# Attention maxima reduced two banks at a time, and a PE order planned with bursts of one key step

## What is computed

```python
att = jnp.einsum('bhql,bhkl->bhqk', q_for_k, k_lat) * L ** (-0.5)
causal = jnp.tril(jnp.ones((T, T), dtype=bool))
att = jnp.where(causal[None, None], att, -jnp.inf)
att = jax.nn.softmax(att, axis=-1)
y_lat = jnp.einsum('bhqk,bhkl->bhql', att, v_lat)
```

## Time and profile before

| | |
|---|---|
| median of 3 runs | 3118.36 us (3117.6 to 3118.45) |
| the profiled execution's own time | 3112.8 us |
| its span | 3111.2 us |
| PE busy / DVE busy / ACT busy, share of the span | 91% / 73% / 60% |
| attention stage | about 462 to 2246 us of the span |
| one slot of it in the steady part | 107 us |

### The profile page before, as it was taken

How to read it: one execution, slowest core, us unless ns; L and a number is a source line. 1 busy time by engine, 2 the same in 40 slices (tenths; PEclk the granted TensorE clock), 3 DMA queues, 4 the chain that set the end, 5 groups by cost and what they waited for, 6 DMA issues and landing times. The chain is left out here.

```text
span 3111.2 us, 50281 instructions
## 1 busy us (share of the span) xinstructions
PE 2844.3 (91%) x16538; PEld 1923.9 (62%) x16538; DVE 2273.6 (73%) x5659; ACT 1858.7 (60%) x3718; POOL 776.4 (25%) x701
## 2 busy tenths in 40 slices
PE   7888957999999999999999999999889997899990
PEld 5677744555555555555555555555367775799990
DVE  7999967888888888888888888888134543445443
ACT  4666632576667666666766676666535443546544
POOL 5777851010000001000110000010024444123220
PEclk9999986899999999999999999999989998899995
DMA  4666674242243234314332432340083220434316
GB/s 153 225 224 223 217 233 105 52 101 54 52 103 78 54 76 97 69 43 102 77 78 52 103 78 54 76 95 14 11 299 117 93 76 20 118 71 109 69 21 223
DMA packets 259647, 320.07 MB, mean 103 GB/s; under 512 B 70578, under 2 KB 157787, under 8 KB 258144
## 3 DMA queue, kind: packets, MB, share of 16 engines
q1 hardware_dynamic: 241760, 294.09, 33.4%
q0 software_dynamic: 17664, 23.19, 3.9%
HBM read 182.76 MB, written 143.95 MB: 105 GB/s over the span
## 5 line engine op out<-in xcount | busy, mean ns | idle before, releaser
L803 ACT ACTIVATE att_probs<-att_score_bank 128x512 f32<-128x512 f32 (+3 forms) x2560 | 1159.0, 551 | 608.5 <-PE att_score_bank L732 600.3
L840 DVE TENSOR_REDUCE att_partial_max<-att_max_bank 128x1 f32<-128x512 f32 x1536 | 1004.9, 687 | 124.3 <-PE att_max_bank L720 118.8
L720 PE MATMUL att_max_bank<-att_k_st,att_q_st 96*128 96x512 f32 (+3 forms) x2560 | 906.4, 389 | 31.8 <-DMA att_ident<-in_ident 20.9
L732 PE MATMUL att_score_bank<-att_q_st,att_k_st 98*128 98x512 f32 (+3 forms) x2560 | 924.5, 390 | 10.1 <-DMA att_q_st<-att_max_rows 7.6
L732 PEld LDWEIGHTS att_score_bank<-att_q_st,att_k_st 98*128 98x128 f32 x2560 | 481.8, 191 | 273.2 <-ACT att_probs L803 145.7
L720 PEld LDWEIGHTS att_max_bank<-att_k_st,att_q_st 96*128 96x128 f32 x2560 | 489.4, 193 | 244.7 <-DVE att_partial_max L840 100.7
L844 DVE CUSTOM_DVE_ANT_0 att_edge_sum<-att_max_bank,att_edge 128x128 f32<-128x128 f32 (+3 forms) x1024 | 482.0, 484 | 165.2 <-PE att_max_bank L720 164.7
L826 POOL TENSOR_SCALAR_AFFINE_SELECT att_probs<-att_probs 128x512 f32<-128x512 f32 x256 | 162.5, 635 | 1615.1 <-ACT att_probs L803 1615.1
L746 PE MATMUL att_acc_bank<-att_probs,att_v_st 128*32 128x512 f32 (+3 forms) x5120 | 544.2, 538 | 1.8 <-POOL att_probs L826 0.9
L210 POOL TENSOR_TENSOR proj_op_low<-proj_turned,proj_op_high 128x512 fp32r<-128x512 f32 x192 | 275.0, 1462 | 59.1 <-ACT proj_op_high L332 58.9
L746 PEld LDWEIGHTS att_acc_bank<-att_probs,att_v_st 128*32 128x32 f32 x5120 | 131.9, 109 | 245.2 <-issue 140.3
(11 more groups left out here) (221 smaller groups left out, 3887.3 us busy)
## 6 DMA issues: line engine op xcount, KB each, us to landing
qk_parts<-proj_parts SPq DMA_DIRECT2D x64, 1024.0 KB, 4.6
att_q_st<-qk_parts SPq DMA_DIRECT2D x192, 256.0 KB, 4.0
att_k_st<-qk_parts SPq DMA_DIRECT2D x192, 256.0 KB, 6.1
v_tokens<-proj_v_tok SPq DMA_DIRECT2D x64, 256.0 KB, 4.4
att_v_st<-v_tokens SPq DMA_DIRECT2D x64, 256.0 KB, 6.9
exp_w<-in_ew SPq DMA_DIRECT2D x16, 1024.0 KB, 8.9
dispatched<-mix_empty_rows SPq DMA_DIRECT2D x8, 1036.0 KB, 14.5
exp_rows<-dispatched SPq DMA_DIRECT2D x16, 518.0 KB, 5.5
```

Of the source, the lines that this page charges most:

```text
L720: nc.tensor.matmul(max_ps[u % MAXB][:, 0:width], q_st[0:3 * L, n % QBUF, j, t * P:(t + 1) * P], k_st[0:3 * L, g % 2, kb, j, 0:width], star ...
L732: nc.tensor.matmul(score_ps[h % SCOREB][:, q0:CH], k_st[:, g % 2, kt // TT, j, (kt % TT) * P:(kt % TT + 1) * P], q_st[:, n % QBUF, j, q0:C ...
L803: nc.scalar.activation(probs[:, k % PROBS, j, q0:CH], score_ps[(HG * k + j) % SCOREB][:, q0:CH], ACT.Exp).then_inc(exped, 1)
L840: nc.vector.tensor_reduce(best, bank[:], AX.X, ALU.max).then_inc(unit_reduced, 1)
```

## The change

Three edits, all in attend and its planner:

1. Units are numbered so that t and t+1 of one head and one key block are neighbours (MU). The 4 banks become 2 tensors of two neighbouring banks each. For a pair off the diagonal, one tensor_reduce over 128x2x512 gives both maxima. It waits until both units are scored, and hands back both banks when it ends. Units on the diagonal keep an instruction each.
2. The planner reckons with that: nothing on VectorE for the even unit, 2 x 512 columns at 960 per us plus 0.075 us for the odd one.
3. BURST and GATHER go from 2 to 1, and the weights of the two backlogs in a weighing's price from 0.3 to 0.1.

```diff
-MU = [(s, c, j, t, kb) for s in range(SLOTS) for c in range(NC) for j in range(HG) for t in range(TT) for kb in range(c + 1)]
+MU = [(s, c, j, t + i, kb) for s in range(SLOTS) for c in range(NC) for j in range(HG) for t in range(0, TT, 2)
+      for kb in range(c + 1) for i in range(2)]
...
-BURST = 2
-GATHER = 2
+BURST = 1
+GATHER = 1
...
-                    price[kind] += 0.5 * few + 0.3 * max(0.0, 1.1 - backlog["unit"]) + 0.3 * max(0.0, 1.0 - backlog["score"])
+                    price[kind] += 0.5 * few + 0.1 * max(0.0, 1.1 - backlog["unit"]) + 0.1 * max(0.0, 1.0 - backlog["score"])
...
-        wait = 0.13 if on_diagonal(u) and ready > self.vector else 0.0
-        self.vector = max(self.vector, ready) + wait + columns / 960 + 0.07
-        self.reduced[u] = self.vector + 0.135
+        if on_diagonal(u):
+            wait = 0.13 if ready > self.vector else 0.0
+            self.vector = max(self.vector, ready) + wait + columns / 960 + 0.07
+            self.reduced[u] = self.vector + 0.135
+        elif u % 2:
+            self.vector = max(self.vector, ready) + 2 * columns / 960 + 0.075
+            self.reduced[u - 1] = self.reduced[u] = self.vector + 0.135
...
-        max_ps = [ps(f"max{i}", [P, CH]) for i in range(MAXB)]
+        max_ps = [ps(f"max{i}", [P, 2, CH]) for i in range(MAXB // 2)]
...
-                nc.tensor.matmul(max_ps[u % MAXB][:, 0:width], q_st[0:3 * L, n % QBUF, j, t * P:(t + 1) * P],
+                nc.tensor.matmul(max_ps[u // 2 % (MAXB // 2)][:, u % 2, 0:width], q_st[0:3 * L, n % QBUF, j, t * P:(t + 1) * P],
...
-            bank = max_ps[u % MAXB]
+            banks = max_ps[u // 2 % (MAXB // 2)]
+            bank = banks[:, u % 2]
             best = partial_max[:, m % 2, j * TT + t, kb:kb + 1]
-            dve.wait_ge(unit_scored, u + 1)
             if kb < c:
-                nc.vector.tensor_reduce(best, bank[:], AX.X, ALU.max).then_inc(unit_reduced, 1)
+                if u % 2 == 0:
+                    dve.wait_ge(unit_scored, u + 2)
+                    nc.vector.tensor_reduce(partial_max[:, m % 2, j * TT + t:j * TT + t + 2, kb], banks[:],
+                                            AX.X, ALU.max).then_inc(unit_reduced, 2)
             else:
+                dve.wait_ge(unit_scored, u + 1)
```

## The result

The changed kernel takes 3277.0 us (3274.7 to 3279.4) against 3118.4 us on the same chip: ratio 1.0509, 95% interval 1.0491 to 1.0527. It is slower, as forecast, but by 159 us and not by 44, and outside the range.

The account below looks back on a forecast made before the run. PE was taken to bound the attention stage, with DVE second. Bursts +65 us less relief of waits 21 us gave +44 us on 3118.4, a forecast of 3162 us, 1.4% slower, range 3130 to 3200 us.

Parts of the forecast that it names:

- What bounds the stage: Attention stage: PE bounds it nearly without a gap, really waiting 3.9 us of a 107.0 us slot; DVE second at 84%.
- The paired reduction: DVE, off-diagonal units: 1.13 us per pair, freeing 3.2 us of DVE a slot, which makes DVE idle longer first of all.
- The bursts: PE's weighings: 34 bursts a slot instead of 22, at 0.34 us each, +4.1 us a slot, 65 us in all.
- The relief of the waits: PE's real waits, 3.9 us a slot, shrink by a third: 1.3 us a slot, 21 us in all.
- the signs: What would show the forecast right; for DVE, gaps behind bursts shrink from 1.4 us to under 0.7, PE not faster.
- the share of the second weighings: PE's weighings: bursts bounded between 22 and 40 a slot, taken as 34, two thirds of the way.
- The step that failed: Loads, stores and SP's issues: they keep their place relative to the scores, no wait against them, nothing booked.
- one to four chunks: Maxima in the attention stage: combined that far ahead of their use, so a delay of the combining steps is hidden.
- Rivals: Four: all alone, pairs hold PE up, 3232 us (0.13); faster, 3081 (0.20); even, 3118 (0.08); dear pair, 3245 (0.02).
- few banks, handed back in twos: Two pairs give DVE at most 2.3 us of stock; both banks return after 1.13 us, the first previously after 0.60.
- The last rival: DVE's paired reduction takes 1.37 us, adding 8 us a slot; PE's waits double, +62 us, giving 3245 us; chance 0.02.

Follow-up runs that it names:

- e2: The changed kernel with each off-diagonal unit reduced by its own instruction, order and numbering kept; 3275.9 us, 1.0502.
- e10: The changed kernel with loads issued earlier (score 12 + 16 c) and single reductions in place of paired ones; 3162.3 us, 1.0142.
- e3: The kernel before, with the second weighing put off by one unit or score in 272 of 289 two-weighing bursts; 3196.1 us, 1.0248.
- e1: The changed kernel with SP issuing the next slot's chunk loads at score 12 + 16 c instead of 12 + 24 c; 3167.6 us, 1.0164.
- e5: The changed kernel with the old BURST, GATHER and backlog weights, but each off-diagonal unit reduced and its bank handed back by itself; 3207.8 us, 1.0276.
- e4: The changed kernel with BURST, GATHER and backlog weights of before (2, 2, 0.3), so pairs alone; 3219.0 us, 1.0323.

## Why the prediction was wrong

- **What bounds the stage: right.** PE; and DVE's 26 us less of busy time went into idle time (e2 and e10 against their partners).
- **The paired reduction: right.** 1.13 us start to start, worth nothing at the end. The page of the Trainium skill that the prediction sets against it ("VectorE: DVE Perf Modes", section "The DRAIN you can't avoid") says in the same paragraph that a next operation which is not held starts earlier. Its rule therefore gave no price for two reductions in a row, and the 0.60 us of the earlier trace rows do not contradict it.
- **The bursts: right in number and price.** 34 a slot were forecast, 35 found; 0.34 us was booked, 0.33 is what the rows of e3 and before show. In steady slots 13 x 0.33 = 4.3 us, where 4.1 stood.
- **The relief of the waits: right.** PE's real waits are 4.6 us a slot before and 3.5 in e1: 1.1 us less, where 1.3 was booked. Waits of DVE did not shrink as the signs had it: in e1 23 pieces of up to 1.0 us are left, not all under 0.7. The sum without the load is +2.8 us a slot by forecast and +3.1 by e1, +44 us by forecast and +48 measured. That the share of the second weighings (two thirds) and of the relief (a third) came out so well is partly luck, since both were guesses between bounds.
- **The step that failed** is the sentence "All loads, stores and SP's issues keep their place relative to the scores, with no wait in the slot's list against them, and I book nothing". It fails twice. Not all of them keep their place: the stores of the maxima's rows hang on the units, and with the lead of the units they moved from score 721 to 674, in front of the load at 676, which then went out 7.8 us late. And the consumer of a load is a unit too, which now comes 12 scores behind it in place of 60. Nothing in the list of waits shows such slack, 32 us before. The term that was put at nothing cost 11 x 10.6 = 116 us by the traces and 109 us by the medians of e1 and the changed kernel. The prediction had even named the units' lead as "one to four chunks" and used it for the maxima alone.
- **Rivals.** None was right. The pairs were rightly suspected to go badly with bursts of two, but e5 shows that the reason given (few banks, handed back in twos) holds for a tenth of the time and a quarter of the steady slot's loss. The last rival's time, 3245, lies nearest, and it would have been nearest for no reason, since the pair takes 1.13 us and not its 1.37.
- **Accounting.** Of the 159 us, 109 are the late load with its half clock (e1 against the changed kernel). 49 are left, or 48 against the kernel before as it was timed beside e1. Of the 48, bursts are 213 x 0.33 = 70 and the relief of the waits is -1.1 x 16 = -18; that makes 52, and the 4 between lie outside the steady slots and were not traced.

## What to carry to other kernels

Where an order is planned, ask for each transfer whether its first consumer moved and what stands in front of it in its queue, and write its slack down as a number before calling it hidden. A change that lets one stream of work run further ahead uses up that slack slowly, so that here the first slots look well. And where the array changes its tiling, count the changes: here each cost PE 0.33 us, and a reduction less frees 0.067 us on an engine that has time.

## What the runs showed of the hardware

Going over from the 128x128 matmuls to the 128x32 weighings and back costs PE 0.33 us at the 2.4 GHz level, and it lies in three places: 0.09 us going in, 0.14 inside the burst, 0.10 at the matmul behind. In e3 0.28 of it reached the end. The Trainium skill, page "TensorEngine Tiling (Array Packing)", section "Key Properties", says that a change of tiling mode drains the engine. The lost time in the rows fits that, though no run parts the tiling from the operands that change with it.

An idle stretch of 8 us on PE brought the granted clock to the 1.2 GHz level, and it stayed there for some 5 us of work behind it: 0.70 in the stretch and 0.50 in the 3.7 us that followed, where e1 has 1.00 there. A wait of 8.3 us so cost 10.6.

It does not take a long stretch without work. In e4 the clock fell to the 1.2 GHz level for 6.8 us in four slots, with no wait of PE over 0.3 us ahead of it: PE was in the run of ten units that wait for banks.

SP's queue works in order. It took 5.0 us to issue eight stores and 3.4 to 4.0 us for seven loads, and the load landed some 6.3 us behind its last issue, at 221 GB/s meanwhile.
